# Expert weights cut into the attention's weight tiles during the last attention steps

## The reference

```python
x = layernorm(x + attention(x, adj, adj))          # 16 heads; scores + 2 * adj; softmax; @ Wo.T
def experts(x, adj):
    top1 = argmax(x.mean(axis=1) @ router_w + router_b)     # one of 4 experts for each graph
    support = x @ expert_w[top1]
    out = adj @ support
    mean, var = per_expert_sums(out, out * out)             # over all graphs of an expert
    return relu((out - mean) * rsqrt(var + eps) * gamma + beta)
x = layernorm(x + experts(x, adj))
```

## Time and profile before

| | |
|---|---|
| runs | 2800.11 us median of 3 (2798.2 to 2800.65) |
| the profiled execution | 2796.44 us, of which the span from first to last instruction is 2794.7 us |
| attention block | up to 2016.0 us |
| expert block | from 2016.0 us to about 2523 us |
| normalisation | from there to the end |
| busy share of the span | PE 96%, PEld 81%, DVE 72%, ACT 54%, POOL 46% |

### The profile page before, as it was taken

How to read it: one execution, slowest core, us unless ns; L and a number is a source line. 1 busy time by engine, 2 the same in 40 slices (tenths; PEclk the granted TensorE clock), 3 DMA queues, 4 the chain that set the end, 5 groups by cost and what they waited for, 6 DMA issues and landing times. The chain is left out here.

```text
span 2794.7 us, 77903 instructions
## 1 busy us (share of the span) xinstructions
PE 2679.6 (96%) x22583; PEld 2263.7 (81%) x22584; DVE 2007.6 (72%) x8351; ACT 1512.3 (54%) x5391; POOL 1277.2 (46%) x1174
## 2 busy tenths in 40 slices
PE   8999999999999999999999999999689999997776
PEld 7888888888888888888888888888578888884232
DVE  6788888888888888888878887888633333334887
ACT  5565555556565656565656565656444444442444
POOL 2333333333333333334333433333256666666887
PEclk9999999999999999999999999999899999998999
DMA  4111111111111111111111111111144444445999
GB/s 146 62 53 53 53 61 53 53 53 61 54 52 56 57 57 49 61 53 57 49 64 51 55 53 61 53 53 53 55 131 133 137 133 137 133 137 189 395 406 348
DMA packets 169427, 277.32 MB, mean 99 GB/s; under 512 B 19378, under 2 KB 52146, under 8 KB 168882
## 3 DMA queue, kind: packets, MB, share of 16 engines
q1 hardware_dynamic: 150962, 243.36, 26.3%
q10 hardware_dynamic: 18432, 33.56, 3.1%
HBM read 184.57 MB, written 92.27 MB: 99 GB/s over the span
## 5 line engine op out<-in xcount | busy, mean ns | idle before, releaser
L512 POOL TENSOR_TENSOR probs<-probs,row_scale 128x512 f32<-128x512 f32 x512 | 532.6, 1040 | 1092.6 <-DVE row_scale L408 1092.4
L316 ACT ACTIVATE probs<-neg_s,neg_max 128x128 f32<-128x128 f32 x2048 | 793.3, 392 | 138.8 <-DVE neg_max L384 138.8
L384 DVE CUSTOM_DVE_ANT_0 neg_s<-att_bank,adj_nat 128x128 f32<-128x128 f32 x2048 | 442.6, 285 | 4.3 <-PE att_bank L197 2.4
L316 ACT ACTIVATION_READ_ACCUMULATOR probs<-neg_s,neg_max 128x1 f32 x2048 | 390.7, 191 | 0.0
L393 DVE TENSOR_REDUCE abs_max<-neg_s 128x4 f32<-128x512 f32 x512 | 349.0, 682 | 0.1
L176 PE MATMUL att_bank<-xt_hi,att_w_hi 128*128 128x256 f32 x2048 | 329.5, 283 | 11.0 <-DVE att_w_lo L366 11.0
L176 PE MATMUL att_bank<-xt_hi,att_w_lo 128*128 128x256 f32 x2048 | 330.0, 283 | 0.0
L176 PE MATMUL att_bank<-xt_lo,att_w_hi 128*128 128x256 f32 x2048 | 329.5, 283 | 0.0
L176 PEld LDWEIGHTS att_bank<-xt_hi,att_w_hi 128*128 128x128 f32 x2048 | 298.9, 191 | 30.5 <-issue 10.6
L344 ACT ACTIVATE probs_t<-att_bank 128x512 f32<-128x512 f32 x256 | 153.1, 598 | 299.3 <-PE att_bank L235 299.2
L176 PEld LDWEIGHTS att_bank<-xt_hi,att_w_lo 128*128 128x128 f32 x2048 | 283.1, 192 | 0.0
(11 more groups left out here) (133 smaller groups left out, 5370.2 us busy)
## 6 DMA issues: line engine op xcount, KB each, us to landing
xt_stage<-in_x_t SPq DMA_DIRECT2D x64, 512.0 KB, 3.5
x_nat<-in_x SPq DMA_DIRECT2D x128, 256.0 KB, 2.6
x_scratch<-x SPq DMA_DIRECT2D x128, 256.0 KB, 2.0
g_x<-x_scratch SPq DMA_DIRECT2D x128, 256.0 KB, 2.8
n_x<-x_scratch SPq DMA_DIRECT2D x128, 256.0 KB, 5.9
out_x<-n_x ACTq DMA_DIRECT2D x128, 256.0 KB, 5.5
y_scratch<-g_out SPq DMA_DIRECT2D x96, 256.0 KB, 2.0
n_y<-y_scratch SPq DMA_DIRECT2D x96, 256.0 KB, 5.6
```

The source lines that it names most:

```text
L316: nc.scalar.activation(probs[:, h * P:(h + 1) * P], neg_s[:, h * P:(h + 1) * P], ACT.Exp, bias=neg_max[:, h:h + 1], scale=-1.0, accum_out= ...
L384: nc.vector.tensor_tensor_reduce(neg_s[:, h * P:(h + 1) * P], bank[r][:, c * P:(c + 1) * P], adj_nat[:, s], -2.0, BIG, ALU.add, ALU.min, n ...
L512: nc.gpsimd.tensor_tensor(part, part, by, ALU.mult).then_inc(probs_done, 1)
```

## The change

- One pair `W_hi`, `W_lo` is shared by attention and expert phase; so are the tiles `g_x1` and `adj_t` (its row is now 160 wide instead of 129, with the same 129 columns used). To make room, most attention tiles become views of `kept`, and the q/k ring becomes `out_sum` and `out_sq`, with the shapes as before.
- SP loads graphs 0 to 3 of the expert phase at attention step 124, expert 2 in step 126 behind that step's x1 store (and behind `e_lo_done` 1), expert 3 in step 127 ahead of the x1 store (behind `e_lo_done` 2), both into `w_stage`.
- ACT cuts expert 0 at the end of step 125, expert 1 at the end of step 126, expert 2 at the end of step 127, expert 3 after the loop.
- DVE makes the rest of expert 0 in step 126 and expert 1 in step 127, ahead of `o_lo`; the rest of expert 2 in step 127 ahead of the wait for the output projection; the rest of expert 3 first thing in the expert block.
- In the expert block PE waits only for two small fills, which POOL now makes at the kernel's start; DVE waits for the three others.

```diff
+            def load_expert_w(e, freed):
+                sp.wait_ge(e_lo_done, freed)
+                sp.dma_start(w_stage[:, e % 2], io["expert_w"][e].rearrange("(c p) k -> p c k", p=P))\
+                  .then_inc(expert_w_in[e], 16)
...
+                if last and t == B - 1:
+                    load_expert_w(3, 2)
                 sp.wait_ge(x1_done, t + 1)
                 sp.dma_start(x1_dram[t], x1[:, s]).then_inc(x1_out[s], 16)
+                if last and t == B - 2:
+                    load_expert_w(2, 1)
+                if last and s == 0:
+                    for g in range(UNROLL):
+                        sp.wait_ge(x1_out[g], 32)
+                        sp.dma_start(g_x1[:, g], x1_dram[g]).then_inc(g_x1_in[g], 16)
+                        sp.dma_start(adj_t[:, g, 0:P], io["adj_t"][g]).then_inc(g_adj_in[g], 16)
...
+            def cut_expert(e, freed, last_use):
+                act.wait_ge(freed, last_use)
+                act.wait_ge(expert_w_in[e], 16)
+                nc.scalar.activation(W_hi[:, e], w_stage[:, e % 2], ACT.Copy).then_inc(e_hi_done, 1)
...
+                if last and t >= B - 3:
+                    e = t - (B - 3)
+                    cut_expert(e, *((qk_ps, 4 * B) if e < V else (v_ps, B)))
             for_steps(act, body)
+            cut_expert(O, wo_ps, B)
...
+            def rest_of_expert(e):
+                dve.wait_ge(e_hi_done, e + 1)
+                nc.vector.tensor_tensor(W_lo[:, e], w_stage[:, e % 2], W_hi[:, e].bitcast(F32),
+                                        ALU.subtract).then_inc(e_lo_done, 1)
...
+                if last and t >= B - 2:
+                    rest_of_expert(t - (B - 2))
                 dve.wait_ge(o_hi_done, t + 1)
...
+                if last and t == B - 1:
+                    rest_of_expert(V)
                 dve.wait_ge(wo_ps, t + 1)
...
-            pe.wait_ge(filled, 5)
-            pe.wait_ge(router_in, 32)
+            pe.wait_ge(ones_done, 2)
             for s in range(2):
                 y_product(s, s, 0)
...
-            rest_of_weights(0)
-            rest_of_weights(1)
-            dve.wait_ge(filled, 5)
+            dve.wait_ge(e_hi_done, E)
+            nc.vector.tensor_tensor(W_lo[:, E - 1], w_stage[:, (E - 1) % 2], W_hi[:, E - 1].bitcast(F32),
+                                    ALU.subtract).then_inc(e_lo_done, 1)
+            dve.wait_ge(filled, 3)
             dve.wait_ge(router_in, 32)
             for s in range(2):
                 part_scores(s, s)
                 y_low(s, s)
             route(0, 0)
-            for e in range(2, E):
-                rest_of_weights(e)
```

More of the change, by code:

```diff
@@ L42, in is_kept, with attention_phase @@
     return s % KEPT_EVERY == KEPT_EVERY - 2
-def attention_phase(nc, io, W_hi, W_lo, w_stage, expert_w_in, ident, x1_dram, B, D):
+def attention_phase(nc, io, W_hi, W_lo, w_stage, expert_w_in, ident, ones, g_x1, adj_t, hand_over, kept, pair,
+                    x1_dram, B, D):
     C = D // P
@@ L197, in scores @@
                         mm = pe.matmul(bank[r][:, c * P:(c + 1) * P],
-                                       qk[rows, par, Q, c, j * P:(j + 1) * P],
-                                       qk[rows, par, K, c, j * P:(j + 1) * P], start=True, stop=True)
+                                       qk[par][rows, Q, c, j * P:(j + 1) * P],
+                                       qk[par][rows, K, c, j * P:(j + 1) * P], start=True, stop=True)
                 mm.then_inc(s_ps, 1)
@@ L309, in copy_qk @@
                 act.wait_ge(qk_ps, n + 1)
-                nc.scalar.activation(qk[:, par, which, c, :], bank[BANK_B][:, 0:GN], ACT.Copy,
+                nc.scalar.activation(qk[par][:, which, c, :], bank[BANK_B][:, 0:GN], ACT.Copy,
                                      scale=HALF_SCALE if which == Q else 1.0).then_inc(qk_done[0], 1)
@@ L496, in _ @@
                 pool.sem_inc(x1_out[s], 16)
+            nc.gpsimd.memset(ones[:, :], 1.0).then_inc(ones_done, 1)
+            nc.gpsimd.memset(adj_t[:, :, P:P + 1], 1.0).then_inc(ones_done, 1)
             nc.gpsimd.memset(minus_half[:, :], -0.5).then_inc(const_done, 1)
@@ L1155, in build, with sem @@
         expert_row = sb("expert_row", [1, B], U32)
[L1157 to L1164, removed]
+        def sem(name):
+            return ctx.enter_context(nc.semaphore(name))
+        e_hi_done, e_lo_done = sem("e_hi_done"), sem("e_lo_done")
+        g_x1_in = [sem(f"g_x1_in{i}") for i in range(UNROLL)]
+        g_adj_in = [sem(f"g_adj_in{i}") for i in range(UNROLL)]
+        ones_done = sem("ones_done")
+        hand_over = e_hi_done, e_lo_done, g_x1_in, g_adj_in, ones_done
         kept = sb("kept", [P, B // KEPT_EVERY, D])
         out_sum, out_sq = sb("out_sum", [P, E, D]), sb("out_sq", [P, E, D])
-        with ExitStack() as inner:
-            W_hi, W_lo = cut_weights("exp_w", inner)
+        with ExitStack() as cut:
+            W_hi = cut.enter_context(nc.sbuf_tensor("w_hi", [P, 4, C, D], F32R))
+            W_lo = cut.enter_context(nc.sbuf_tensor("w_lo", [P, 4, C, D], F32R))
+            g_x1 = cut.enter_context(nc.sbuf_tensor("g_x1", [P, UNROLL, D], F32))
+            adj_t = cut.enter_context(nc.sbuf_tensor("adj_t", [P, UNROLL, P + P // 4], F32))
+            attention_phase(nc, io, W_hi, W_lo, w_stage, expert_w_in, ident, ones, g_x1, adj_t, hand_over, kept, (out_sum, out_sq),
+                            x1_dram, B, D)
             expert_phase(nc, io, W_hi, W_lo, w_stage, expert_w_in, ones, expert_row, kept, out_sum, out_sq,
-                         x1_dram, y_dram, B, D, E)
+                         g_x1, adj_t, hand_over, x1_dram, y_dram, B, D, E)
         norm_phase(nc, io, ident, ones, expert_row, kept, out_sum, out_sq, x1_dram, y_dram, out_dram, B, D, E)
```

52 lines of the change are left out of this document (13 added, 39 removed).

## The result

| | before | changed |
|---|---|---|
| median | 2796.45 us (20 runs) | 2792.48 us (20 runs) |
| ratio of the runs | 1 | 0.9984, 95% interval 0.9977 to 0.9991 |
| profiled execution's span | 2794.7 us | 2791.9 us |

The kernel became faster, by 0.16%, or 4.5 us (2.5 to 6.4 by the interval), where 6.7 were forecast. The forecast time, 2793.4, lies 0.9 from the median, but that is partly luck: the three runs of before that it started from had a median of 2800.11, and twenty have 2796.45. The gain is the number to judge by, and it falls short by a third.

What follows compares the result with a forecast made beforehand. TensorE is busy throughout the attention loop; the switch to experts is a hole, ended by waits for POOL's fill and DVE's cuts. 18.87 - 9.4 - 2.8 = 6.7 us saved gives 2793.4 us, range 2789.6 to 2797.8.

Steps and rivals of the forecast that it cites:

- Where the change acts: Switch from attention to experts: a hole in TensorE's work, and the change acts there alone; the loop's 1901.5 us stay.
- rival 4: Attention loop: the tiles' new places make each of 128 steps longer; at 0.12 us a step 2808.8 us; chance 0.07.
- rival 5: Expert block: another wait holds the first product to its old place; 2800 us, no gain; chance 0.05.
- The later phases unchanged: Sign to look for in the changed kernel: the phases after the first expert product stay as they were.
- B moves by 2.8 us: End of attention: DVE's rest of expert 2 waits for its load, so the expert block starts 2.8 us later, at 2018.8.
- the quiet row: Expert 2's load in step 126: a quiet 1 MB expert weight load lands in 5.3 us (4.8 to 7.4).
- Rival 1: End of attention: the DVE wait costs nothing, expert 2 is cut before 2010.4; gain 9.5, 2790.6 us; chance 0.05.
- Rival 2: End of attention: loads of experts 2 and 3 share the transfer, both landing near 2012; gain 3.9, 2796.2 us; chance 0.10.
- First product at B + 9.4: Expert block: first expert product starts 9.4 us behind block start B instead of 18.87, a gain of 9.5.
- Rival 3: Expert block: POOL's fills stretch by the subtraction's 2.29 us, routing starts later; gain 4.4, 2795.7 us; chance 0.10 with late router weights.
- TensorE back at full clock within the first product: First expert product: part of the upper bound, gain 8.1; it ran 1.97 where 1.17 is seen at full clock.
- The likeliest class: Whole kernel: faster by more than 0.2% (5.6 us), given 0.62; within 0.2% was given 0.31, slower 0.07.

Runs made afterwards that it cites:

- e2: Changed kernel with DVE's rest of expert 2 moved behind x1 of graph 127; ratio to the kernel before 0.9975.
- e3: Changed kernel with SP issuing expert 2's load ahead of the x1 store of step 126 instead of behind it; ratio to the kernel before 0.9972.
- e8: Changed kernel with early expert 2 load, expert 3's rest behind x1, DVE awaiting one fill, idle products (52, 10, 4); 2786.31 us, 0.9966 of before.
- e10: As e8, with 44 instead of 52 idle products behind the last output projection; 2785.50 us, ratio to the kernel before 0.9960.
- e6: Changed kernel with DVE waiting for POOL's first fill alone instead of all three; 2791.57 us, ratio to the kernel before 0.9982.
- e5: Changed kernel with idle TensorE products: 52 after the last projection, 10 after graphs 0 and 1, 8 after router_scores; ratio to the kernel before 0.9976.
- e1: Changed kernel run again, unedited; ratio to the kernel before 0.9984.
- e9: Kernel before the change profiled again, unedited; 3.71 us from the first expert product to graph 3's product.
- e7: Changed kernel with graphs 0 to 3 loaded in the expert block again, graph 0 ahead of the router weights; ratio to the kernel before 0.9992.

## Why the prediction was right or wrong

1. **Where the change acts**: right for attention. The x1 store of step 126 is issued at 2003.14 and 2001.78 in the profiles of the kernel before, at 2002.78 and 2001.57 in those of the changed kernel, so rival 4 (slower steps) is out; rival 5 is out too, since the long waits went. "The later phases unchanged" was wrong by 1.2 us: from graph 3's product to the start of the last pass of the last expert product it is 490.3 us in both profiles of before, and 491.2 to 491.6 in all ten of the changed kernel and its variants. Why is not shown. The prediction put the new places of the tiles at nothing; no run sets these, or the wider row of `adj_t`, apart.
2. **B moves by 2.8 us**: right in mechanism (e2, e3), a little small: 16.06 - 12.90 = 3.2. The term that was off is the load, 5.3 us by the quiet row. It took 5.9 in the first profile, and 5.4 to 5.9 in the seven profiles that have it in the same place; 5.0 to 5.3 in e3, e8 and e10. In the seven it follows a 256 KB store by 0.39 us, and the load of expert 3 follows it by 3.0; no run tells which of the two slows it. The fit that the prediction takes from the Trainium skill, "DMA: Bandwidth & Descriptors", "Anatomy of one DMA", 4.4 us, is below all of these; the page gives it for DMAs that GpSimd issues, and SyncE issued these. Rival 1 is out. Rival 2 too: ACT's cuts of experts 2 and 3 start 3.7 us apart, not together.
3. **First product at B + 9.4**: measured 9.81. The fills hold the routing as forecast (e6), and part_scores started 4.09 behind the block for 3.95; the routing was 0.2 faster; the reading of the expert's number, taken as 0.8, took 2028.68 - 2027.39 = 1.29 (1.20 to 1.29 in e5, e6 and e8). Rival 3 is out: fills of 1.81 and 1.80 us ran beside the subtraction of 2.29 (from 2019.20), all unstretched. The conflict that the prediction takes from the Trainium skill, "Advanced Engine Details and Errata", "GPSIMD Details", did not show here for a fill, which has no input.
4. **The step that failed**: the sum ended at the *start* of the first expert product and took the product itself over from before, with only a gain in view ("TensorE back at full clock within the first product"). It took 5.15 us up to graph 3's product instead of 3.69, a loss of 1.5. What the prediction counted as 0.8 us of reading is a pause in TensorE's work, or the end of one. In e1 and e6 the clock falls in that pause, in the first profile it has not risen ahead of it; e5 shows that with idle products in the holes 2.2 us come back, e9 that before there was no such pause. The Trainium skill, "TensorE: Matmul & The Clock Gate", Part 1, says that the array's clock has two levels and is gated by how busy the array has recently been. Granted 1.00, 0.72 and 0.50 in e6's three windows agree, 0.72 being the mean of a stretch with both levels in it.
5. **The sum**: 6.7 forecast; 6.7 - 0.4 - 0.4 - 1.5 = 4.4 with the first three corrections, and 3.2 with the expert loop's 1.2. The ratio gives 4.5 (2.5 to 6.4) and can't tell the two apart. That rival 3 also said 4.4 is coincidence; what it named did not happen. The direction and the range held. Two ends of the working are slightly off, without weight for the result: 0.5 and 0.8 more make the upper gain 8.0, not 8.1, and a gain of 3.0 with 1 us of spread ends the range at 2798.1, not 2797.8. The likeliest class did not hold: 0.16% lies within the 0.2% that I gave 0.31, since the forecast stood only 1.1 us above that bound.

## What to carry to other kernels

A hand-over that moves work ahead of a barrier must move its loads far enough ahead: an instruction waiting for a late load at the head of an in-order queue delays everything behind it, here the residual, the last store and the barrier. Sum to the first point where both kernels run alike again, not to the start of the first instruction: a pause that a long wait used to cover left the first product here at half clock. And a wait on a shared counter is worth reading: DVE waited for two fills that only POOL needed, 1.55 us for one digit.

## What the runs showed of the hardware that I had not expected

- In e1, e6 and e7 the product of graph 2 ran at full clock, TensorE then idled for 2.3 us, and nearly all of the next 5.0 to 5.3 us ran at half clock. In e2 and e3 the clock fell already within the product of graph 2. With idle products ahead it stayed at full through pauses of 0.6 to 1.1 us (e5, e8, e10). These runs have both more work ahead and shorter pauses, so they do not tell which of the two kept the clock up.
- A 1 MB load issued 0.39 us behind a 256 KB store, with another megabyte issued 3.0 us behind it, landed in 5.4 to 5.9 us, and in 5.0 to 5.3 with neither (e3, e8, e10). Which of the two costs is not shown.
